# Attention in a two-layer adaLN kernel: the transposes of the split row maxima, and ScalarE's copy of them, in the fourth slot of each group in place of the third

## The reference, cut to what matters

```python
q = (x @ W_q.T).reshape(B, S, H, dk).transpose(0, 2, 1, 3)     # H = 16 heads of dk = 8
k = (x @ W_k.T).reshape(B, S, H, dk).transpose(0, 2, 1, 3)
v = (x @ W_v.T).reshape(B, S, H, dk).transpose(0, 2, 1, 3)
q = apply_rope(q)
k = apply_rope(k)
scores = jnp.einsum('bhqd,bhkd->bhqk', q, k) / jnp.sqrt(jnp.asarray(dk, x.dtype))
scores = jnp.where(causal, scores, jnp.asarray(-jnp.inf, x.dtype))
probs = jax.nn.softmax(scores, axis=-1)
attn = jnp.einsum('bhqk,bhkd->bhqd', probs, v)
```

## Time and profile before

| | before |
|---|---|
| runs, us | 579.49, 581.68, 581.73 (median 581.68) |
| profiled execution, us | 577.07 (span of the trace 575.2) |
| PE busy | 452.4 us (79%), 3120 instructions |
| PE weight loads | 274.4 us (48%) |
| DVE busy | 392.0 us (68%) |
| ACT busy | 278.1 us (48%) |
| POOL busy | 271.6 us (47%) |
| mean granted PE clock | 0.889 |

### The profile page before, as it was taken

One profiled execution on the slowest core, in us unless ns is written; L12 is line 12 of the kernel. 1 busy time (PEld: TensorE's weight loads), 2 busy tenths in 40 slices (PEclk: granted clock), 3 DMA queues, 4 the chain that ended last, 5 costly groups with the idle time before them and its releaser, 6 DMA issues.

```text
span 575.2 us, 10088 instructions
## 1 busy us (share of the span) xinstructions
PE 452.4 (79%) x3120; PEld 274.4 (48%) x3120; DVE 392.0 (68%) x1264; ACT 278.1 (48%) x518; POOL 271.6 (47%) x392
## 2 busy tenths in 40 slices
PE   3688778987998999994558998999999863059970
PEld 3545456766653444442323434435445343049970
DVE  5789738988655888886679687888898235025533
ACT  1568796653453544441223577678777831013220
POOL 4210038998301786664641047476655502714541
PEclk9988889999799999997775799999999985559995
DMA  8600000000335333310386012222300000141114
GB/s 354 169 1 1 0 2 2 1 2 1 144 148 125 99 106 99 107 62 2 108 208 124 4 31 88 82 86 85 84 5 4 3 0 10 52 123 36 36 38 146
DMA packets 25739, 39.94 MB, mean 69 GB/s; under 512 B 3228, under 2 KB 17756, under 8 KB 25164
## 3 DMA queue, kind: packets, MB, share of 16 engines
q1 hardware_dynamic: 21752, 30.42, 17.8%
q0 software_dynamic: 3936, 8.89, 5.2%
HBM read 27.55 MB, written 11.55 MB: 68 GB/s over the span
## 4 chain that ended last, share of the span: by engine, by line
PE 49%; DVE 18%; POOL 11%; issue 8%; ACT 6%; DMA 6%; SPq 0%; DVEq 0%; POOLq 0%; ACTq 0%
PE ps L1579 5%; PE ps L1581 5%; PE ps L1568 5%; PE ps L1686 4%; PE ps L1599 3%; PE ps L1771 3%; PE ps L1782 3%; POOL slots_x L586 3%; DVE rows L406 3%; PE ps L1391 2%; DVE moe L1221 2%; PE ps L1641 2%; POOL qk_parts L305 2%; DVE st L387 2%; PE ps L1672 2%
## 5 line engine op out<-in xcount | busy, mean ns | idle before, releaser
L1221 DVE CUSTOM_DVE_ANT_0 moe<-ps,const 128x512 bf16<-128x512 f32 (+3 forms) x256 | 110.5, 486 | 9.7 <-PE ps L1641 9.4
L778 ACT ACTIVATE arena<-ps 128x256 f32<-128x256 f32 (+3 forms) x128 | 85.8, 701 | 33.6 <-PE ps L1672 32.9
L476 POOL TENSOR_TENSOR arena<-arena 128x512 f32<-128x512 f32 x32 | 51.7, 1616 | 51.9 <-DVE arena L1139 51.7
L1641 PE MATMUL ps<-arena 48*128 48x128 bf16 (+3 forms) x256 | 56.1, 329 | 10.7 <-DVE arena L1221 4.7
L1672 PE MATMUL ps<-arena 51*128 51x128 bf16 (+3 forms) x256 | 52.2, 307 | 0.0
L1686 PE MATMUL ps<-arena 128*32 128x512 f32 (+3 forms) x512 | 48.4, 450 | 0.9 <-ACT arena L778 0.6
L1667 PE MATMUL ps<-bconst 64*128 64x64 bf16 x512 | 45.6, 195 | 1.2 <-ACT arena L778 0.5
L1641 PEld LDWEIGHTS ps<-arena 48*128 48x128 bf16 x256 | 16.7, 97 | 55.7 <-DVE arena L1221 31.7
L751 ACT ACTIVATE arena<-arena 128x512 f32<-128x512 f32 x32 | 20.2, 630 | 41.9 <-DVE arena L1139 41.6
L838 ACT ACTIVATE arena<-ps 128x512 f32<-128x512 f32 x23 | 13.7, 597 | 55.0 <-PE ps L1771 55.0
L592 POOL DMA_INDIRECT tokens_y<-arena,token_at x23 | 22.1, 960 | 32.5 <-DVE arena L1325 31.3
(11 more groups left out here) (239 smaller groups left out, 1113.2 us busy)
## 6 DMA issues: line engine op xcount, KB each, us to landing
arena<-expert_weights SPq DMA_DIRECT2D x32, 256.0 KB, 3.2
arena<-moe_in SPq DMA_DIRECT2D x1, 4100.0 KB, 12.8
qk_parts<-arena SPq DMA_DIRECT2D x24, 128.0 KB, 2.3
qk_parts<-arena POOLq DMA_DIRECT2D x24, 128.0 KB, 2.3
arena<-qk_parts POOLq DMA_DIRECT2D x32, 96.0 KB, 2.5
arena<-qk_parts SPq DMA_DIRECT2D x8, 288.0 KB, 5.6
moe<-moe_in SPq DMA_DIRECT2D x1, 1936.0 KB, 13.8
slots_x<-zeros SPq DMA_DIRECT2D x1, 1518.0 KB, 19.6
```

Of the source, the lines that this page charges most:

```text
L476: pool.tensor_tensor(yacc[:, ts], yacc[:, ts], pr[:, i % 2, :], ALU.add).then_inc(sem("yacc"), 1)
L778: act.activation(pt[:, u % 4, :, 0:n], ps[:, 4 + 2 * k:6 + 2 * k, 0:n], ACT.Exp, scale=ATT_SCALE).then_inc(sem("probs"), 1)
L1221: v.tensor_tensor_reduce(out=junk[:, done % 2, 0:n], in0=ps[:, k, col:col + n], in1=w["mask"][:, (3 - qt) * P:4 * P], scale=1.0, scalar=3 ...
L1641: mm = pe.matmul(ps[:, k, col:col + n], qaug[lo:lo + KR, b % 2, 2 * g + j // 2, qt * P:(qt + 1) * P], kaug[lo:lo + KR, b % 2, 2 * g + j // ...
```

## The change

PE's `maxima_T(it + 1)` moves from behind slot 2's `scores_T` to behind slot 3's `scores_T`, ahead of that slot's `weighted_values`. ACT's copy and the ring's entry move from slot 2 to slot 3 too. Nothing is added or removed.

```diff
@@ -277,7 +277,7 @@
                 if it + 2 < 16:
                     for n in at_slot[i]:
                         ring.append((("mx", it + 2, n), ("mx", 16 * (it + 2) + maxima_done[n + 1])))
-                if i == 2 and 0 <= it + 1 < 16:
+                if i == 3 and 0 <= it + 1 < 16:
                     ring.append((("mT", it + 1), ("mT", it + 2)))
                 if i == 3 and 0 <= it - 1:
                     ring.append((("oT", it - 1), ("at", it)))
@@ -1726,10 +1726,10 @@
                             scores(it + 2, u)
                     if 0 <= it < 16:
                         scores_T(8 * it + i)
+                    if i == 3 and 0 <= it + 1 < 16:
+                        maxima_T(it + 1)
                     if i % 2 == 1 and 0 <= 4 * it + i // 2 - 1 < 64:
                         weighted_values(4 * it + i // 2 - 1)
-                    if i == 2 and 0 <= it + 1 < 16:
-                        maxima_T(it + 1)
                     if i == 3 and 0 <= it - 1:
                         o_T(it - 1)
                     if i == 5 and it >= 4 and it % 4 == 0:
```

## The result

| | before | changed |
|---|---|---|
| median, us (17 runs each) | 578.8 (576.7 to 581.73) | 575.54 (573.22 to 577.55) |
| ratio of the times | | 0.9936, 95% interval 0.9918 to 0.9955 |
| profiled execution: span, us | 575.2 | 572.5 |
| PE busy, us | 452.4 | 446.3 |
| mean granted PE clock | 0.889 | 0.885 |

The changed kernel is 0.64% faster, 3.7 us by the ratio. The forecast was 0.58 us faster. The base moved too: with 17 runs the median of before is 578.8 us, where the three runs shown ahead had 581.68. With that base the forecast would have been 578.2 us, 2.7 us above what came; 2.9 of the 5.6 us between the forecast of 581.1 and the measured median are this move of the base.

The account below looks back on a forecast made before the run. PE was taken to bound the attention, DVE close behind. Terms -1.01 - 1.01 + 0.48 + 0.19 + 0.29 + 0.48 = -0.58 us took the median from 581.68 to 581.1 us; 8 in 10 range 578.4 to 583.6.

Parts of the forecast that it names:

- What bounds the kernel: In the attention, PE sets the pace with DVE close behind; iteration 1 has PE busy 8.77 of 9.17 us.
- PE's work stays the same. The move swaps these two blocks.: On PE, u3 with slot 3's scores_T comes 0.32 us earlier and the transposes 0.49 us later, with unchanged work.
- The gain in POOL's waits: PE works while POOL is late: 1.01 us gained in iterations 3 and 4, 1.01 in 7, 8 and 10.
- u4's wait: u4 waits for DVE's reading of u3: 0.48 us in iteration 5, 0.19 in 13, none net in 9.
- And nowhere else: Expected trace sign: u4 waits for DVE in iterations 5, 9 and 13 only.
- The start: In iteration -1 the transposes move behind u3: first scores_T 0.52 us late, 0.29 left after iteration 0's idle 0.23.
- signs of being wrong: Middle-iteration waits for L364's DMA, u4 waits in more than three iterations, or PE's clock rising at another place.
- My rival: The clock rises one iteration later, so iteration 1 looks like iteration 0: +2.4 us, 583.5; chance 0.06, half each side.
- The end: The last group's copy moves behind slot 3's probs and the second pass waits for its DMA: 0.48 us cost.
- The rows in time: The maxima's rows land 0.47 us later but stay hidden in middle iterations; iteration 11 keeps 0.43 of 0.90 us.
- The term that I put at zero: The cost of the later copy and DMA of the maxima's rows between first and last iteration: zero.
- the rival with the late rows: The copy falls back a whole slot, 1.43 us, so rows come late: about +3.5 us, 585.2; chance 0.10.

Follow-up runs that it names:

- copy_slot2: The changed kernel with ACT's copy of the maxima alone back in slot 2, ahead of slot 3's probs: 575.59 us, 0.9942 of before.
- stats_slot4: The changed kernel with DVE's statistics of iterations 5, 9 and 13 at slots 4 and 6, not 2 and 4: 574.69 us, 0.9931 of before.
- only_iteration0_at_3: The kernel before with iteration 0 alone moved to slot 3 (transposes, copy and ring): 578.86 us, 0.9995 of before.
- ends_slot2: The changed kernel with transposes, copy and ring entry of iterations -1 and 14 back in slot 2: 574.98 us, 0.9922 of before.

## Why the prediction was wrong

- **What bounds the kernel** held: PE, with DVE close behind.
- **"PE's work stays the same. The move swaps these two blocks."** This is the step that failed. I priced u3's block at 0.49 and the transposes at 0.32 us from the earlier trace rows, each by the next instruction's start, and took these prices along to the new order, as if the neighbours' prices stayed. But 0.49 is what a piece of 64-row work costs with 128-row work behind it. u3's block still has that behind it and takes 0.48 (420.86 to 421.34); it is slot 2's block ahead of it, u2 with its `scores_T`, that now has its own kind behind it and went from 0.49 (423.66 to 424.15) to 0.30 (420.56 to 420.86). And the transposes with `weighted_values` take 0.57 us together, where they took 0.32 + 0.35 before; they now stand next to work over the same 128 rows. In iteration 11 the two savings are 0.19 + 0.10 us, less some hundredths that u4 waits. The same place filled with 64-row and 128-row matmuls, 0.41 against 0.82 us, shows that it is the form that costs. The iterations 1, 11 and 12, which never waited for POOL, gained 0.28, 0.34 and 0.28 us, where I had zero; 2 and 6 gained only 0.04, with DVE done with u3 no earlier against u2 than before and u4 waiting for it.
- **The gain in POOL's waits** was right in mechanism, and the sizes agree by luck. The iterations 3 and 4 gave 1.09 us (1.01 forecast), but as 0.26 and 0.83 where I had 0.49 and 0.52. From u2 to u4 iteration 3 gained 0.58 us (346.57 to 349.94 before, 345.91 to 348.70 now); the late rows took 0.32 of it back in front of iteration 4. The cheaper order, which I didn't have, is in both iterations. The iterations 7, 8 and 10 gave 0.48 + 0.63 + 0.60 = 1.71, where I had 1.01; PE's cheaper order is in these iterations too, and POOL's chain from `part_hi` to iteration 10 was not as fixed as I took it; how the 0.70 us divide between the two was not tested, and iteration 10 alone varies by 0.4 us between kernels with the same order there. `part_hi` 0.5 us earlier is shown by `copy_slot2`.
- **u4's wait** was right in iteration 5 and in size near (0.64 by `stats_slot4`, 0.48 forecast; 0.14 and 0.13 for 9 and 13, none and 0.19 forecast). "And nowhere else" was wrong: it binds in eight iterations, because PE now reaches u4 sooner, and caps what the cheaper order gives.
- **The start**: 0.61 us by the table, 0.52 forecast ahead of the cover. Iteration 0 was to give back 0.23; it gave 1.58. Of that 0.89 came ahead of u4 at 1.2 GHz. Start and iteration 0 up to u4 together took 24.07 us before, 23.79 now, and 23.42 in both kernels with the start in slot 2 and iteration 0 in slot 3 (`only_iteration0_at_3`, `ends_slot2`). So the start's move cost 0.37 us, where I had 0.29, and iteration 0's gave 0.65, POOL's wait and the order together. The other 0.70 goes with the clock's earlier rise, which moving iteration 0 alone turned off and on in the traces (0.72 and 0.50 us from L1599 on). My rival had the clock rise later, and priced a whole iteration.
- **The end**: 0.48 us forecast, 0.48 measured (7.12 to 7.60), and undone by `ends_slot2`. The chain of the changed kernel still runs through it:

```profile
450.14 1.71 DMA arena<-arena
451.85 0.05 issue
451.90 0.23 PE ps L1667 x4
```

- **The rows in time** did not hold everywhere, and this was one of my signs of being wrong. In iteration 11 they did, but only just: the copy came 0.47 us later against u2, as forecast (1.11 us before, 1.58 now). Since PE also got faster, SP's last issue ends 1.15 us ahead of the reader, with 1.11 needed at the last group: 0.04 us to spare, where I had 0.43. In iteration 3 the rows came 0.32 us late. I had taken 1.70 us from issue to landing, the last group's, for all groups, and iteration 11 for one of the tightest; behind iteration 3 it took about 2.4. The term that I put at zero cost 0.3 us there and at most 0.1 in iteration 7. With this, all three signs of being wrong that I named came: a wait for the DMA of L364 in the middle, waits of u4 in more than three iterations, and a clock that rises at another place.
- A slip in the sum of the rival with the late rows: half of 13 x 0.53 with 2.86 and -2.02 is +4.3 us and not +3.5, so its time would be 586.0 us. It changes no bound.

The sum by terms, from the table: 0.61 for the start, -1.58 for iteration 0, -1.09 for 3 and 4, -1.71 for 7, 8 and 10, -0.98 for 1, 2, 6, 11 and 12, +0.29, +0.09 and +0.08 for 5, 9 and 13, +0.48 for the end: -3.81 us. 0.70 us of it is the clock, which one trace can't give to the median.

## What to carry to other kernels

The price of a block of matmuls, read as the distance to the next instruction, belongs to its neighbours too: ask whether the order sets matmuls over part of the array's rows next to such over all of them, and group them by kind before looking for waits. Where an ordering change saves time in iterations that waited for nothing, look at the gaps of the instructions on either side of the moved one, not at the semaphores. A move in a ring of banks changes who waits for whom; how often the new wait binds has to be judged at the new pace, not at the old one. And a DMA's time to landing is to be read in each stretch in which it has to be hidden: the last group's 1.7 us did not hold for iteration 3.

## What the hardware showed that I had not expected

- Four transposes over 128 rows, at 2.4 GHz, cost 0.51 us between two pieces of 64-row work (0.30 to 0.81 us from u2 to u3), and 0.22 us up to the next ones beside other 128-row work.
- Four matmuls of 128 columns and 64 rows between the same pieces cost 0.11 us, those with 128 rows 0.52 us, at the same clock, though one of them takes 0.22 us either way.
- Transposes with 12 output columns and matmuls with 32 output columns, both over 128 rows, ran in among each other: L1651's last started 0.05 us behind the first of L1686.
- SP's four small DMAs were there 1.7 us behind the last one's issue at the last group, and about 2.4 us behind it in iteration 3, where POOL issued three DMAs of its own in the meantime; the cause was not tested.
- A change of one iteration's order, at 1.2 GHz, went together with a low-clock stretch of 23.9 in place of 27.3 us, in ten traces of fourteen against four.
